# Four neighbouring tokens per partition, and the triangle's result stored token by token, in a two-layer pair kernel on one core

## What is computed

```python
# layer 0: triangle multiplication
x = layernorm(pair, ln1_w, ln1_b)
left  = sigmoid(x @ left1)  * (x @ left2)
right = sigmoid(x @ right1) * (x @ right2)
p = einsum('nsre,nkre->nske', left, right)      # for each feature e a 128 x 128 x 128 product over r
p = layernorm(p, ln2_w, ln2_b)
q = einsum('nrse,ez->nsrz', p, out_w) * sigmoid(x @ gate)
pair = pair + q
# layer 1
left = pair @ W_left + b_left + pair @ W_eq + b_eq
right_sum = sum over r of (pair @ W_right + b_right)
out = (left * right_sum * sigmoid(pair @ W_gate + b_gate)) @ W_out + b_out
return layernorm(out + pair, ln_scale, ln_bias)
```

## Time and profile before

| what | us |
|---|---|
| median of three runs | 113.91 |
| the profiled execution: span from first to last instruction | 112.1 |
| PE busy, DVE busy, ACT busy, POOL busy in that span | 92.5, 77.3, 66.6, 62.6 |

### The profile page before, as it was taken

One profiled execution on the slowest core, in us unless ns is written; L12 is line 12 of the kernel. 1 busy time (PEld: TensorE's weight loads), 2 busy tenths in 40 slices (PEclk: granted clock), 3 DMA queues, 4 the chain that ended last, 5 costly groups with the idle time before them and its releaser, 6 DMA issues. The chain is left out here.

```text
span 112.1 us, 1886 instructions
## 1 busy us (share of the span) xinstructions
PE 92.5 (83%) x600; PEld 72.3 (64%) x600; DVE 77.3 (69%) x284; ACT 66.6 (59%) x110; POOL 62.6 (56%) x78
## 2 busy tenths in 40 slices
PE   1997599789999899999979999999999996495000
PEld 1994368567776799545445789878877994394000
DVE  1528697986769800599975869699979963996500
ACT  0614888687785166795499463993797399330000
POOL 5037974599950040025488585587865492699400
PEclk9999999999999999999999999999999999999955
DMA  3669997000000000000000000000023006029996
GB/s 60 126 111 171 146 146 75 0 0 0 0 0 9 0 0 0 0 0 3 0 0 0 3 6 0 0 0 6 0 35 59 0 0 94 0 34 144 147 144 100
DMA packets 33486, 4.54 MB, mean 40 GB/s; under 512 B 33348, under 2 KB 33476, under 8 KB 33476
## 3 DMA queue, kind: packets, MB, share of 16 engines
q1 hardware_dynamic: 31632, 4.00, 27.6%
q10 hardware_dynamic: 1844, 0.41, 1.8%
HBM read 2.31 MB, written 2.10 MB: 39 GB/s over the span
## 5 line engine op out<-in xcount | busy, mean ns | idle before, releaser
L596 DVE TENSOR_TENSOR lr<-bank,sig_lr 128x512 f32<-128x512 f32 x16 | 15.9, 1044 | 3.7 <-ACT sig_lr L431 3.7
L817 PE MATMUL bank<-lr_blk,xnT 64*128 64x256 f32 x128 | 16.5, 392 | 1.0 <-ACT xnT L421 0.7
L352 POOL TENSOR_TENSOR t_tok<-p_sb,rstd 128x512 f32<-128x512 f32 x7 | 10.2, 1462 | 11.8 <-DVE rstd L666 11.8
L360 POOL TENSOR_TENSOR x_low<-x1T,x_high 128x512 fp32r<-128x512 f32 x8 | 10.3, 1290 | 7.5 <-ACT x_high L501 7.5
L817 PEld LDWEIGHTS bank<-lr_blk,xnT 64*128 64x128 f32 x128 | 11.8, 186 | 4.0 <-issue 2.3
L660 DVE BATCH_NORM_STATS2 stats<-p_sb 128x6 f32<-128x64 f32 x64 | 8.5, 211 | 7.0 <-ACT p_sb L465 7.0
L368 POOL TENSOR_TENSOR oT<-o_a,rsum 128x512 f32<-128x512 f32 x8 | 8.7, 1089 | 6.4 <-DVE o_a L706 4.2
L431 ACT ACTIVATE sig_lr<-bank 128x512 f32<-128x512 f32 x16 | 9.6, 598 | 3.9 <-PE bank L817 3.9
L581 DVE BATCH_NORM_STATS2 stats<-x_tok 128x6 f32<-128x64 f32 x64 | 8.9, 213 | 3.5 <-DMA x_tok<-in_x 3.3
L978 PEld LDWEIGHTS bank<-wout_blk,oT 128*128 128x128 f32 x64 | 8.1, 191 | 4.0 <-POOL oT L368 3.2
L978 PE MATMUL bank<-wout_blk,oT 128*128 128x128 f32 x64 | 8.8, 281 | 2.2 <-POOL oT L368 2.2
(11 more groups left out here) (104 smaller groups left out, 199.8 us busy)
## 6 DMA issues: line engine op xcount, KB each, us to landing
x_tok<-in_x SPq DMA_DIRECT2D x14, 128.0 KB, 4.2
out<-sq SPq DMA_DIRECT2D x7, 256.0 KB, 3.4
x_tok<-in_x SPq DMA_DIRECT2D x3, 64.0 KB, 2.7
w_rep<-in_weights ACTq DMA_DIRECT2D x1, 180.5 KB
out<-sq ACTq DMA_DIRECT2D x1, 128.0 KB, 3.7
out<-sq SPq DMA_DIRECT2D x1, 128.0 KB, 3.8
x_tok<-in_x ACTq DMA_DIRECT2D x1, 64.0 KB, 2.7
row_rep<-in_rows ACTq DMA_DIRECT2D x1, 32.0 KB, 5.1
```

The lines of the kernel that those rows point to most:

```text
L352: nc.gpsimd.tensor_tensor(place(t_tok[:, c % 2], 0, SPC), even_first(p_sb[:, :, s]), even_first(rstd[:, 1:2, s]).to_broadcast([P, 2, SPC / ...
L360: nc.gpsimd.tensor_tensor(x1_low[:, c % 2], x1T[:, c % 3], x1_high[:, c % 2], ALU.subtract).then_inc(x1_low_ready, 1)
L596: nc.vector.tensor_tensor(lr[:, :, s].rearrange("p f s -> p s f"), src[:, :, 2 * CH:4 * CH], sig_lr[:, j % 3].rearrange("p (s f) -> p s f" ...
L817: last = nc.tensor.matmul(dst, xnT[half, c, k * P:(k + 1) * P], lr_blk[half].rearrange("p g m c -> p g (m c)"), start=True, stop=True, ski ...
```

## The change

A partition now holds four neighbouring tokens of r: partition (b, q) with b = s mod 4 and r = 4q + m; along it lie chunk, slot t and m, where s = 4(4 chunk + t) + b. So a run in DRAM is four tokens, 512 bytes, for the loads into `x_tok` and for the stores. `xc` is written with m outermost, so that a transpose takes one m at a time (`xc_of`), and its columns come out by block b. The statistics of chunk 0 are still summed in two halves, but root, transpose and affine take the whole chunk. For the residual x is loaded a second time, in 128-byte runs, into the memory of `sq` (`x_res`, laid out by m), and the loop's transposes of x read that. The left and right factors lie in pairs: the columns of `lr_blk` are (feature, slot) with two slots innermost, and `multiply_lr` is two instructions, each of 64 features by two pairs, that write two neighbouring words of `lr`. The copy of p reads a bank token by token and writes `p_sb` with the four features of a token side by side, and `statistics2` and the normalising read it packed. The loop's other steps keep their count and only address their columns by block.

```diff
-SUMS1 = [(0, 8), (8, 16)] + [(16 * n, 16 * n + 16) for n in range(1, 8)]
-ROOTS1 = [(0, 8), (8, 16), (16, 32), (32, 48), (48, 64), (64, 96), (96, 128)]
-TURNS = [(0, 8), (8, 16)] + [(16 * n, 16 * n + 16) for n in range(1, 8)]
-OWN_CENTRE = 1
+RM = 4
+SLOTS = SPC // RM
+HALF = SPC // 2
+SUMS1 = [(0, HALF), (HALF, SPC)] + [(16 * n, 16 * n + 16) for n in range(1, 8)]
+ROOTS1 = [(0, 16), (16, 32), (32, 48), (48, 64), (64, 96), (96, 128)]
+OWN = 1
...
-    x_tok_dram = x[0].rearrange("s r c -> r s c")
-    out_tok_dram = out[0].rearrange("s r c -> r s c")
+    def runs(dram):
+        return dram[0].rearrange("(k t b) (q m) c -> k (b q) t (m c)", k=CHUNKS, t=SLOTS, m=RM)
+    x_runs, out_runs = runs(x), runs(out)
+    x_by_m = x[0].rearrange("(k t b) (q m) c -> k (b q) m t c", k=CHUNKS, t=SLOTS, m=RM)
...
-        xc = sb("xc", [P, P, CH])
+        xc = sb("xc", [P, CHUNKS, RM, COLS // RM])
...
-        p_sb = sb("p_sb", [P, CH, P])
+        p_sb = sb("p_sb", [P, P, CH])
...
+        x_res = sq[:].rearrange("p s c -> p (s c)").rearrange("p (k m j) -> p k m j", k=CHUNKS, m=RM)
...
+        def xc_of(lo, hi):
+            slots = slice(lo % SPC // RM, (hi - 1) % SPC // RM + 1)
+            return xc[:, lo // SPC].rearrange("p m (t c) -> p t m c", t=SLOTS)[:, slots]
...
+        def scale_t(engine, c):
+            return engine.tensor_tensor(t_tok[:, c % 2],
+                                        p_sb[:].rearrange("p (b q) e -> p b q e", b=BLK)
+                                        [:, :, c * SLOTS:(c + 1) * SLOTS],
+                                        of_chunks(rstd[:, 1], c, c + 1).rearrange("p b (q a) -> p b q a", a=1)
+                                        .to_broadcast([P, BLK, SLOTS, CH]), ALU.mult)
...
-                for first in range(lo, hi, SPC):
-                    last = min(first + SPC, hi)
-                    for n in range(2 if b else 1):
-                        sp.dma_start(place(x_tok[:], first, last)[:, n], x_tok_dram[:, first + n:last:2, :]
-                                     ).then_inc(x_in[b], 16)
+                c, t = lo // SPC, lo % SPC // RM
+                n = (hi - lo) // RM
+                sp.dma_start(x_tok[:, lo:hi, :].rearrange("p (t m) c -> p t (m c)", m=RM), x_runs[c][:, t:t + n]
+                             ).then_inc(x_in[b], 16)
+            for c in range(CHUNKS):
+                sp.dma_start(x_res[:, c].rearrange("p m (t c) -> p m t c", t=SLOTS), x_by_m[c]).then_inc(x_again, 16)
+            def store(c):
+                s = slice(c * SPC, (c + 1) * SPC)
+                return sp.dma_start(out_runs[c], sq[:, s, :].rearrange("p (t m) c -> p t (m c)", m=RM))
             for c in range(CHUNKS - 1):
-                s = slice(c * SPC, (c + 1) * SPC)
                 sp.wait_ge(final, c + 1)
-                sp.dma_start(out_tok_dram[:, s, :], sq[:, s, :]).then_inc(x_out, 16)
-            s = slice(P - SPC // 2, P)
+                store(c).then_inc(x_out, 16)
...
             pool.wait_ge(consts, 1 + 2 * GRP)
+            centre(1)
             pool.wait_ge(w_in, 16)
             nc.gpsimd.tensor_tensor(lr_blk[:],
-                                    w_rep[:, 0:4 * CH].rearrange("p (a m c) -> p a m c", a=1, m=4)
-                                    .to_broadcast([P, 2, 4, CH]),
-                                    pair_mask[:].rearrange("p g (a c) -> p g a c", a=1).to_broadcast([P, 2, 4, CH]),
+                                    w_rep[:, 0:4 * CH].rearrange("p (f a) -> p f a", a=1)
+                                    .to_broadcast([P, 4 * CH, 2]),
+                                    pair_mask[:].rearrange("p (a g) -> p a g", a=1).to_broadcast([P, 4 * CH, 2]),
                                     ALU.mult).then_inc(lr_blk_ready, 1)
-            centre(1)
             normalise1(1)
...
-            act.dma_start(place(x_tok[:], lo, hi)[:, 1], x_tok_dram[:, lo + 1:hi:2, :]).then_inc(x_in[0], 16)
...
             root1_of(0)
-            root1_of(1)
             act.wait_ge(w_in, 16)
             affine1(0)
+            root1_of(1)
             root1_of(2)
+            sigmoid_lr(0, 0)
             affine1(1)
-            root1_of(3)
-            sigmoid_lr(0, 0)
+            sigmoid_lr(0, 1)
             affine1(2)
-            sigmoid_lr(0, 1)
-            affine1(3)
             sigmoid_lr(1, 0)
             sigmoid_lr(1, 1)
-            for b in (4, 5, 6):
+            for b in (3, 4, 5):
                 root1_of(b)
             sigmoid_lr(2, 0)
-            affine1(4)
+            affine1(3)
...
-                src = bank[:, b].rearrange("p (e s) -> p e s", e=4)
-                nc.scalar.activation(p_sb[:, 4 * b:4 * b + 4, :], src, ACT.Copy).then_inc(p_ready, 1)
+                src = bank[:, b].rearrange("p (e s) -> p s e", e=4)
+                nc.scalar.activation(p_sb[:, :, 4 * b:4 * b + 4], src, ACT.Copy).then_inc(p_ready, 1)
...
             def multiply_lr(c, h):
                 j = 2 * c + h
-                s = slice(c * SPC + h * SPC // 2, c * SPC + (h + 1) * SPC // 2)
                 lo = 2 + 2 * (j % 3)
-                src = bank[:, lo:lo + 2].rearrange("p b (s f) -> p (b s) f", f=4 * CH)
+                dst = lr[:].rearrange("p f (n h k t g) -> p n h k t f g", n=2, h=2, k=CHUNKS, t=2)
+                src = bank[:, lo:lo + 2].rearrange("p t (n w f g) -> p n w t f g", n=2, w=2, g=2)
+                sig = sig_lr[:, j % 3].rearrange("p (t n f g) -> p n t f g", t=2, n=2, g=2)
                 dve.wait_ge(lr_sig, j + 1)
-                nc.vector.tensor_tensor(lr[:, :, s].rearrange("p f s -> p s f"), src[:, :, 2 * CH:4 * CH],
-                                        sig_lr[:, j % 3].rearrange("p (s f) -> p s f", f=2 * CH),
-                                        ALU.mult).then_inc(lr_ready, 1)
+                for n in range(2):
+                    last = nc.vector.tensor_tensor(dst[:, n, h, c], src[:, n, 1], sig[:, n], ALU.mult)
+                last.then_inc(lr_ready, 1)
...
             statistics1(0)
+            statistics1(1)
             lo, hi = SUMS1[0]
             dve.wait_ge(stats1_ready, 1)
-            nc.vector.tensor_tensor(place(xc[:], lo, hi), place(x_tok[:], lo, hi), mean_of(lo, hi), ALU.subtract
+            nc.vector.tensor_tensor(xc_of(lo, hi), token(x_tok[:, lo:hi, :]), token(mean_of(lo, hi)), ALU.subtract
                                     ).then_inc(centre0, 1)
             inverse1(0)
             dve.wait_ge(centre0, 1)
             dve.wait_ge(rstd1, 1)
-            nc.vector.tensor_tensor(place(xc[:], lo, hi), place(xc[:], lo, hi),
-                                    each_feature(rstd[:, 0], lo, hi), ALU.mult).then_inc(xn_ready, 1)
-            statistics1(1)
+            nc.vector.tensor_tensor(xc_of(lo, hi), xc_of(lo, hi), token(each_feature(rstd[:, 0], lo, hi)), ALU.mult
+                                    ).then_inc(xn_ready, 1)
+            statistics1(2)
             inverse1(1)
-            statistics1(2)
+            statistics1(3)
             inverse1(2)
-            statistics1(3)
-            inverse1(3)
             statistics1(4)
             multiply_lr(0, 0)
             statistics1(5)
...
+                for b in range(BLK):
+                    for t in range(0, SLOTS, 2):
+                        k = (b * CHUNKS + c) * SLOTS + t
+                        last = nc.vector.bn_stats(stats2[:, k:k + 2, :].rearrange("p s v -> p (s v)"),
+                                                  p_sb[:, k:k + 2, :].rearrange("p s c -> p c s"))
...
+                if c == 0:
+                    pe.wait_ge(xn_ready, 1)
+                pe.wait_ge(xn_pool, c + 1)
+                if c >= 2:
+                    pe.wait_ge(xnT_ready, c - 1)
+                by_m = bank[:, c % 2].rearrange("p (b m q) -> p m b q", b=BLK, m=RM)
+                for m in range(RM):
+                    last = nc.tensor.transpose(by_m[:, m], xc[:, c, m], ident[:])
...
+                        b = 2 * n + h
+                        last = nc.tensor.matmul(bank[:, 2 + 2 * (j % 3) + t, n * COLS // 2:(n + 1) * COLS // 2],
+                                                xnT[half, c, b * P:(b + 1) * P],
+                                                lr_blk[half].rearrange("p f g -> p (f g)"),
...
             project_lr(0, 0)
+            project_lr(0, 1)
             transpose_xn(1)
-            project_lr(0, 1)
+            project_lr(1, 0)
             transpose_xn(2)
-            transpose_xn(3)
-            project_lr(1, 0)
             project_lr(1, 1)
...
+                    pe.wait_ge(x_again, 16 * CHUNKS)
+                for m in range(RM):
+                    last = nc.tensor.transpose(bank[:, XT, m * P:(m + 1) * P], x_res[:, c, m], ident[:])
```

More of the change, by code:

```diff
@@ L415, in root1_of, with affine1 @@
                 root(0, lo, hi, root1)
-            def affine1(n):
-                lo, hi = TURNS[n]
-                c = lo // SPC
-                act.wait_ge(xnT_ps, n + 1)
```

(20 more changed lines are left out.)

169 lines of the change are left out of this document (63 added, 106 removed).

## The result

The changed kernel takes 109.15 us (median of 4 runs, 108.95 to 109.58) against 113.97 us (4 runs, 113.77 to 114.5) on the same chip: a ratio of 0.957, interval 0.950 to 0.963. The forecast was 108.7, its range 106.8 to 112.2. The profiled run took 109.12 us, its span 107.2 us against 112.1. So the total came out, but not by its terms. These are the places where the two spans part. A gain is by how much earlier the changed kernel is there; the last column is what the forecast had gained by then.

What follows compares the result with a forecast made beforehand. PE was taken to bound the middle and loop, x's statistics the start, the stores' rate the end. Gains 3.5 + 1.5 + 0.2 + 0 = 5.2 us gave 108.7 us, range 106.8 to 112.2.

Steps and rivals of the forecast that it cites:

- The tail: End of the kernel: 512-byte stores run at 215 instead of 145 GB/s, so the last lands earlier; gain 3.5 us.
- The start: Up to the last statistics of x: fewer packets remove waits, a later T costs some back; gain 1.5 us.
- Rival 3: The start gives nothing: weights land at 7.29 or later, every chunk stands behind ACT's affine; 110.2 us, chance 0.17.
- The two waits for x go: In the start: with a quarter of the packets, DVE's waits of 1.96 and 0.63 us for x's transfers vanish.
- T: Start of chunk 0's first transposes, forecast at 7.65 us; the last statistics were to end at T + 11.3 = 18.95.
- PE's clock granted at 1.00 as long as PE works: Expected sign: TensorE keeps its full granted clock whenever it works, as in the stages before the change.
- The new wait behind the affine step: In the start: ACT's root of chunk 1 follows chunk 0's affine, so DVE's second reciprocal waits 2 us or more.
- The products: DVE's left-right products: written in pairs, two halves take 0.85 us together instead of 1044 ns; gain 0.2 us.
- once, at the last product before the triangle: In the PE-bound middle stage, the products' 0.2 us gain was to show only at this one place.
- The evacuation: ACT's copies of the triangle's banks go from 0.60 to 0.96 us, costing 0.36; DVE's first t regains 0.36; net 0.
- Rival 1: The evacuation becomes the bound: at three times 0.60, 1.79 us a bank, the time is 115.3 us; chance 0.11.
- The loop: The PE-bound loop from 62 to 92 us: POOL's packed t and the new orders were costed at nothing.

Runs made afterwards that it cites:

- the first experiment: The changed kernel with its stores alone back in 128-byte runs: 111.35 us, against 109.15 us for the changed kernel.
- the two lists: On the changed kernel with four weight loads, ACT's root of chunk 1 put before chunk 0's affine, POOL's scaling of chunk 0's half before lr_blk: 105.83 us.

## Why the forecast was right in its total, and where not

*The tail* (3.5 forecast, 4.0 measured). Right in its mechanism, too small in its rate: I took 215 GB/s, and the stores run at mostly 280 to 310, so no backlog is left. By the Trainium skill (DMA: Bandwidth & Descriptors, Specifications) it was to be near 4.3, and the gain lies nearer to that than to mine, though the rate stays well under the page's 16 times 27 GiB/s. What was wrong is that run length is the reason for all of it: the first experiment gives it 2.2 to 2.8 us of the 4.0, and where the rest comes from stays open. When the last store goes out is now set by POOL's row of five additions: with DVE's done 1.4 us earlier it went out no earlier (the run with TensorE's scaled products ahead). The 2.87 us behind that are the last stores' own.

*The start* (1.5 forecast, -0.2 measured at the first sigmoid of chunk 2). This is the step that failed. Rival 3's outcome came true, not its reason: POOL did not wait for the weights. "The two waits for x go": the one of 0.63 went, the one of 1.96 became 2.25 us, and one of 0.46 came up at chunk 1. I had put both waits down to the number of packets. With the weights in four loads the half's wait is gone, so it was the weights' single load that held it; that the two crowd the same few engines is argued from the busy share and not seen engine by engine. Behind the late half POOL centred it, built lr_blk and scaled it in single file, so T came at 8.74, 1.1 us late. "PE's clock granted at 1.00 as long as PE works" failed as well: this left TensorE idle for 2.05 us, and the lower clock behind that took some 0.8 us. The sum behind T held for the statistics (T + 11.05 measured, T + 11.3 forecast) but not for ACT. Its second load of the roots' table, at 19.02 where it stood at 17.51 before, and not the statistics, was last: they ended 0.73 us earlier than before and the sigmoid behind them 0.19 later. The new wait behind the affine step was named rightly. It showed 0.78 us here, because other things were late too, and 2.14 with the weights out of the way; taking it out, with POOL's order, gave 1.4 us.

*The products* (0.2). Pairs were costed at 0.85 us and measured at 0.69 to 0.83, a full cure. That this shows "once, at the last product before the triangle" failed: 0.5 us between the first sigmoid of chunk 2 and the triangle (15.68 before, 15.18 after), and undoing them cost 0.56 there, since TensorE's last projections wait for the products too.

*The evacuation* (net 0, measured 0.29 of gain at the first x1T). DVE's price for jumps was the wrong row to stand in for ACT: 0.60, not 0.96. Rival 1 is out. The Trainium skill (ScalarE: Activation LUTs, What ACT_TABLE_LOAD costs) names no pattern, and its figures give an estimate of 612 ns; the 597 agree.

*The loop* (0, measured 0.28 of gain from the first x1T to DVE's last addition). It was put at nothing because it is PE's. With the old `p_sb` this gain is gone (50.49 us against 50.22), so it belongs to the layout of p; POOL's t, 1.12 instead of 1.46, lies in that stretch.

*What was costed at nothing*: the second load of x, rightly.

So an error of 1.7 us in the start was made good by 0.5 in the tail and some 0.9 in the middle: that the total came out within half a microsecond is luck.

## What to carry to other kernels

Before a wait for a transfer is put down to its own packets, look at the mean busy share of the DMA engines in that stretch: a low share with a full queue can point to another load, one that is spread over few of them, and cutting that load gave more here (1.9 us, some 0.8 of it by the clock) than anything in x's own layout did for the start. When steps are joined so that one waits longer, price the clock of TensorE behind the wait as well as the wait. A good total is no proof of its terms; compare the two traces point by point.

## What was not expected of the hardware

- The clock's fall is not the same in every execution of the same instructions: behind a wait of 2.05 us it was 0.50, behind 1.68 us in the run with the old p_sb 1.00. Near the end, behind a wait of 1.59 us, it held in the changed kernel and fell to 0.50 with four loads (96 to 98 us).
- DVE's additions from SBUF to SBUF take 1.93 us a pair while POOL's additions run, and 0.75 once these are over (the run with the longer warm-up). The Trainium skill (Trainium Architecture — The Big Picture, What this means for kernel authors) says that these two share a port under a lock; the rows agree.
- ACT reads PSUM in steps of 512 bytes in the time of a packed read, 597 ns for 512 values a partition; DVE pays 0.36 us for writes 512 bytes apart, and nothing that can be seen once they come in pairs.
- The changed kernel with four loads and the two lists takes 105.83 us, 7% less than the kernel before and 3% less than the changed one; with the scaled products ahead it is 105.78, the same.
